# Bounding and masking the probabilities of the masked pairs in one VectorE instruction instead of two

## The reference

```python
scores = jnp.einsum('bhqd,bhkd->bhqk', q, k)          # q, k: 128 latent + 64 rotary
scores = jnp.clip(scores, -80.0, 80.0)
scores = jnp.where(causal[None, None], scores, -jnp.inf)
weights = jax.nn.softmax(scores / jnp.sqrt(jnp.float32(d_qk)), axis=-1)
attn = jnp.einsum('bhqk,bhkd->bhqd', weights, v)
out = attn.transpose(0, 2, 1, 3).reshape(B, S, H * D_H) @ W_O.T
```

## Time and profile before

| | |
|---|---|
| runs before, median of 3 | 1464.39 us (1462.96 to 1464.65) |
| the profiled execution's own time | 1462.57 us |
| its span | 1461.1 us |
| PE busy | 1387.2 us (95%), 9808 matmuls |
| DVE busy | 1173.1 us (80%), 1400 instructions |
| ACT busy | 769.9 us (53%) |
| POOL busy | 111.5 us (8%) |
| DVE, masked pairs: bounding L1177, mask L1181 | x64 each |

### The profile page before, as it was taken

The page is one execution under the profiler, slowest core; times in us unless marked ns, Lnnn a source line. Parts: engine busy times, 40 slices in busy tenths (PEclk is TensorE's granted clock), DMA queues, the critical chain, the costliest instruction groups (busy, mean ns, idle before and its releaser), DMA issues. The chain is left out here.

```text
span 1461.1 us, 27912 instructions
## 1 busy us (share of the span) xinstructions
PE 1387.2 (95%) x9808; PEld 1119.4 (77%) x9808; DVE 1173.1 (80%) x1400; ACT 769.9 (53%) x840; POOL 111.5 (8%) x150
## 2 busy tenths in 40 slices
PE   5999689999999999999999999999999999599998
PEld 4888567778777878787888878888788788378887
DVE  4666388898898898989889898898788798576764
ACT  3322356656666656565566655656655566432221
POOL 0000111101001000000010000000100000112211
PEclk9999899999999999999999999999999999899999
DMA  6423565544525333333242422422421611345652
GB/s 252 144 76 98 176 181 163 155 146 121 150 83 144 95 116 81 124 84 124 58 122 85 124 83 58 122 83 64 124 61 54 227 57 55 120 124 160 178 173 87
DMA packets 111949, 172.77 MB, mean 118 GB/s; under 512 B 9224, under 2 KB 68904, under 8 KB 109096
## 3 DMA queue, kind: packets, MB, share of 16 engines
q1 hardware_dynamic: 97528, 111.10, 24.6%
q0 software_dynamic: 13552, 59.60, 14.0%
q10 hardware_dynamic: 832, 1.57, 0.5%
HBM read 123.75 MB, written 48.50 MB: 118 GB/s over the span
## 5 line engine op out<-in xcount | busy, mean ns | idle before, releaser
L1094 ACT CAST prob_h<-prob 128x1024 fp32r<-128x1024 f32 (+1 forms) x288 | 289.6, 1005 | 271.8 <-DVE prob L1175 198.1
L1194 DVE TENSOR_TENSOR prob_l<-prob,prob_h 128x1024 fp32r<-128x1024 f32 (+1 forms) x288 | 335.9, 1166 | 39.6 <-ACT prob_h L1094 38.2
L1088 ACT ACTIVATE prob<-score_ps 128x1024 f32<-128x1024 f32 (+1 forms) x288 | 282.2, 980 | 149.1 <-PE score_ps L947 103.6
L947 PE MATMUL score_ps<-q_h,key_slot 64*128 64x512 f32 x1792 | 357.0, 392 | 3.7 <-DMA key_slot<-keys 3.5
L969 PE MATMUL out_ps<-prob_h,value_slot 64*128 64x512 f32 (+1 forms) x1792 | 341.7, 378 | 6.7 <-DVE prob_l L1194 5.1
L1189 DVE TENSOR_TENSOR total<-total,prob 128x1024 f32<-128x1024 f32 (+1 forms) x256 | 294.8, 1152 | 0.0
L969 PEld LDWEIGHTS out_ps<-prob_h,value_slot 64*128 64x128 f32 x1792 | 170.4, 184 | 54.9 <-DVE prob_l L1194 17.5
L1175 DVE TENSOR_SCALAR prob<-prob 128x1024 f32<-128x1024 f32 x224 | 155.1, 692 | 66.5 <-ACT prob L1088 66.5
L947 PEld LDWEIGHTS score_ps<-q_h,key_slot 64*128 64x128 f32 x1792 | 170.6, 184 | 43.6 <-issue 6.5
L947 PE MATMUL score_ps<-q_l,key_slot 64*128 64x512 f32 x896 | 177.3, 390 | 0.0
L947 PE MATMUL score_ps<-rot_hh,key_slot 64*128 64x512 f32 x896 | 177.2, 389 | 0.0
(11 more groups left out here) (193 smaller groups left out, 2022.7 us busy)
## 6 DMA issues: line engine op xcount, KB each, us to landing
key_slot<-keys SPq DMA_DIRECT2D x144, 256.0 KB, 2.7
value_slot<-values SPq DMA_DIRECT2D x144, 128.0 KB, 2.0
rows<-heads_rows SPq DMA_DIRECT2D x32, 512.0 KB, 5.9
rot_hh<-turned POOLq DMA_DIRECT2D x30, 512.0 KB, 6.1
heads_rows<-head_rows POOLq DMA_DIRECT2D x15, 1024.0 KB, 10.1
turned<-rot_hl POOLq DMA_DIRECT2D x14, 1024.0 KB, 5.1
rot_l<-turned POOLq DMA_DIRECT2D x30, 256.0 KB, 7.8
wo<-in_w_o POOLq DMA_DIRECT2D x1, 4096.0 KB, 13.0
```

What stands on the lines that cost most here:

```text
L947: mm = pe.matmul(score_ps[:, half, c * 512:(c + 1) * 512], keys_of[ROWS[r], :], moving[par][ROWS[r], half * HW + c * 512:half * HW + (c + ...
L1088: nc.scalar.activation(prob[half][:, 0:width], score_ps[:, half, 0:width], ACT.Exp, scale=QK_SCALE).then_inc(exp_done, 1)
L1094: nc.scalar.copy(prob_h[half][:, 0:width], prob[half][:, 0:width]).then_inc(high_done, 1)
L1194: nc.vector.tensor_tensor(p_l, p, p_h, ALU.subtract).then_inc(split, 1)
```

## The change

In CORNER and LATE pairs the bounding and the mask become one instruction: `scalar_tensor_tensor` computes min(max(p, P_MIN), limit), where `limit` is `keep.causal` broadcast over the four heads. For this `keep.causal` is filled with P_MAX instead of 1.0, so that it holds P_MAX where a key is seen and 0 where it is masked; min with it bounds from above and masks at once. In CORNER the instruction runs over all 256 tokens of each head (1024 columns), in LATE over the 128 tokens there are (512 columns). The semaphore `bounded` and the wait on it go. FULL pairs keep L1175.

```diff
-            nc.gpsimd.memset(keep.causal[:, :], 1.0).then_inc(cleared, 1)
+            nc.gpsimd.memset(keep.causal[:, :], P_MAX).then_inc(cleared, 1)
...
-        bounded = sem("bounded")
...
-                nc.vector.tensor_scalar(p, p, P_MIN, P_MAX, ALU.max, ALU.min).then_inc(bounded, 1)
-
-                dve.wait_ge(bounded, 4 * n + (2 if kind == LATE else 0) + half + 1)
-                masked = by_head(half, kind)[:, :, 0:P]
-                nc.vector.tensor_tensor(masked, masked, keep.causal[:, 0:P].unsqueeze(1).to_broadcast([P, HH, P]),
-                                        ALU.mult).then_inc(clipped, 1)
+                tokens = P if kind == LATE else CT
+                heads = by_head(half, kind)
+                limit = keep.causal[:, 0:tokens].unsqueeze(1).to_broadcast([P, HH, tokens])
+                nc.vector.scalar_tensor_tensor(out=heads, in0=heads, scalar=P_MIN, in1=limit,
+                                               op0=ALU.max, op1=ALU.min).then_inc(clipped, 1)
```

## The result

Ten runs of each kernel: median 1464.89 us before, 1459.11 us after. The ratio on record is 0.9955 (95% interval 0.9945 to 0.9965), 6.6 us less (5.1 to 8.1); the two medians are 5.8 us apart. Forecast were 7.4 us less and 1457.0 us.

What follows compares the result with a forecast made beforehand. PE was taken as the bound, with DVE's time counting only where PE stands still for it. The terms 3.4 + 3.6 + 0.4 = 7.4 us gave a median of 1457.0 us, range 1451.5 to 1461.5.

Steps and rivals of the forecast that it cites:

- Rivals B: The fused instruction runs at two columns a cycle, 692 ns in CORNER, giving 1453 us; chance 0.05.
- C: The fused instruction runs at half the rate, CORNER halves taking 2.29 us instead of 1.42, giving 1488 us; chance 0.03.
- Units 4 to 13: Ten units gain 0.36 us each, 3.6 us, through LATE's earlier halves and DVE's earlier row of work.
- the stop in LATE: PE's wait for `prob_l` in LATE's weighing, units 4 to 13, costing 0.34 us; it was to go.
- the large stop: PE's wait for `prob_l` at FULL k = 1 to 2, units 4 to 13; to end 0.35 us earlier, not much shorter.
- the CORNER saving is worth nothing by itself: In units 4 to 13 CORNER's 0.19 us a half brings nothing: PE is in the latent queries, DVE has pauses.
- Units 0 to 4: Few or no FULL pairs, at the pace of DVE and transfers: 3.4 us gained, bounds 1.3 and 5.5.
- The first term: Unit 0's CORNER and LATE halves, ahead of `split_turned`, become ready earlier, so unit 2 starts 1.27 us earlier.
- The smaller terms: CORNER in units 2 to 4 gives 1.1 us, DVE's lead in unit 2 0.4, LATE of units 2 and 3 0.34 and 0.2.
- Units 14 and 15: Latent queries behind CORNER come 0.38 us earlier in unit 14; unit 15's gain is lost at a key tile; 0.4 us.
- Rival A: Another wait hides the LATE gain in units 4 to 13: 4 us, 1460.4, or 2 us, 1462.4; chance 0.16.
- Rival D: Every 0.9 us that LATE saves in ten units moves the large stop: 12.8 us, 1451.6; chance 0.07.

Runs made afterwards that it cites:

- corner_split: The changed kernel, but CORNER uses two instructions on different columns, bounding the unmasked 512 and fused on the masked 512, with no wait; ratio 0.9964 against the kernel before.
- turn_on_act: The changed kernel with the rounding of the rotated queries moved from DVE to ACT in units 2 to 13; ratio 0.9906 against the kernel before.
- before_turn: The kernel before, without the fused instruction, with the rounding of the rotated queries moved from DVE to ACT in units 2 to 13; ratio 0.9948.
- after_weights: The changed kernel with the last phase's two weight loads issued later in unit 15, behind the store of unit 14's heads; ratio 0.9944 against the kernel before.
- before_again: The kernel before, unchanged, run once more for its profile alone; one run, 1467.17 us.
- before_weights: The kernel before with the last phase's two weight loads issued later in unit 15, behind the store of unit 14's heads; ratio 0.9998.
- corner_only: The kernel before with the fused instruction in CORNER pairs alone, LATE keeping two instructions with the wait; ratio 0.9992.

## Why the prediction was right, point by point

- **The instruction.** 1226 and 692 ns taken, 1224 and 684 measured. Rivals B (692 ns) and C (2290 ns) are out. The rows that decided between them were the two-input instructions and the small scalar_tensor_tensor of the earlier trace rows.
- **The wait between the two instructions.** The pair took 0.73 us from start to start in CORNER; two of that length without a wait between them are 0.61 apart. corner_split has the same at 512 columns: 0.34 us from start to start for a 0.42 us instruction, where before, with the wait, it was 0.45. So the trace disagrees once more with the rule of the Trainium skill (VectorE: DVE Perf Modes, "The DRAIN you can't avoid") that a semaphore costs nothing extra there. By that rule the sum was about 6 us. The interval of the measured time holds that too, so the rows decide it and not the whole time.
- **Units 4 to 13.** Forecast 3.6 us, measured 4.2 in the changed kernel, of which LATE alone is 3.7. The steps are shown: the stop in LATE goes, the large stop comes 0.33 us sooner and is no shorter, and it follows DVE's work (turn_on_act, before_turn). What I sized wrong is "the CORNER saving is worth nothing by itself": it is worth 1.5 us alone, in the odd units, and 0.5 beside the LATE saving.
- **Units 0 to 4.** Forecast 3.4 us. Between executions whose clock stayed up in unit 2, before took 116.35 us, after 112.97 and after_weights 112.31: 3.4 and 4.0 us less. The first term can be read by itself, as the end of `split_turned` of unit 0 after the first key tile. It was 25.88 us in before_again, before_weights and before_turn, 24.55 in after: 1.33 us, forecast 1.27. With LATE alone it was 24.95 (0.93 less). Before itself (25.20) and corner_only (24.80), both with less half clock at the start of unit 0 (3.0 us, 5.2 to 6.2 in the others), are 0.40 apart. These are the 2 x 0.45 and 2 x 0.19. Unit 2's first score matmul then came 40.29 us after the first key tile in after, 42.55 in before_again, 2.3 us sooner where 1.3 was forecast. What is more than 1.3 lies in the transfers (the store landed 5.1 us after its issue instead of 5.6), and they scatter: PE's wait for the queries was 1.8 to 3.0 us in the four profiles without the change and 1.7 to 3.2 in the seven with the whole change, so it can't be said to have fallen. The wait for `total` at the first sums did fall, from 1.7 to 3.0 us to 0 to 1.3; after, PE, as the earlier trace rows:
```profile
196.69 1.06 PE L901 MATMUL out_ps<-total,ones 128*32 128x512 f32 x8 [0.28 <-DVE total L1187]
```
  The smaller terms (1.1 for CORNER in units 2 to 4, 0.4, 0.34 and 0.2) are not confirmed one by one.
- **Units 14 and 15.** 0.4 us forecast for unit 14; the profiles with the change show 114.2 to 115.1 against 114.6 to 115.4, a scatter as large as the term. A gain within unit 15 is lost at the key tile: in its CORNER pair PE stood 1.63 us instead of 1.94, and then for the tile, whose load had been issued before that.
- **Rival A** took place in part: in even units PE now meets the key tile of k = 1 (the row at 512.50). It cost nothing, as argued, since DVE had begun its row of work. **Rival D** is out: the large stop gave back 0.33 us a unit, not 0.9.
- **The sum.** 7.4 us against 6.6 (5.1 to 8.1). Up to unit 15's sums the traces say more than that: 3.4 us (like clock with like), 4.2 and 0.4 (the means of the column 14-15, 115.1 and 114.7) are 8.0. Some 1.4 us seem to be given back behind them, or nothing, as the interval goes. Here the prediction put down nothing: "`combine` and the end are untouched". But "rest" is 209.94 us in after, and 209.5 in the mean of the seven profiles with the whole change (six of them 208.8 or more), against 208.0 to 208.5 in the four without it. So that the sum came within 1 us has some luck in it: units 4 to 13 were sized 0.6 too low, and what is lost behind was left out. The first waits of `combine` show it, after:
```profile
PEld merge_ps L1362 <- DVE merged_l L1462: 16.6, 5, 14.7
...
DVE rows L1420 <- POOL scale L1355: 30.7, 8, 12.3
```
The longest of them were 12.7 and 10.3 us before. They hang on the first transfers of `combine`, and over the seven profiles with the whole change they scatter (rest 208.1 to 211.6 us). Whether the change lengthens them, or the wait in unit 15, is open; no run was made for it.
- **The signs named in advance.** Counted from the first key tile, the sums of unit 5 came 3.9 us sooner in after than in before (3.7 forecast), those of unit 14 7.4 us (7 forecast).

## What to carry to other kernels

Two dependent instructions of an engine that is not the bound are worth fusing where a chain through that engine ends in a stop of the bound; count the stops, not the busy time. Of 18 us that DVE was relieved of, a third came through. Where the engine then works without a pause up to a later stop, that stop gives back what the start of its work gained (0.33 us here), and an instruction taken out between the two can count in full: one 0.69 us copy, moved to an engine with room, brought 7.3 us in the ten units in which the whole fusion brought 4.2. Before a difference between two profiles is put down to a change, take the unchanged one a second time, and compare stretch by stretch, each with its granted clock.

## What the runs showed of the hardware

- Here a burst delayed a small transfer that was issued after it. With the 4 MB load issued 5.1 us ahead, the 256 KB key tile of unit 15 landed 11.7 us after its issue in after (11.8 in before_again, 10.3 in before), where the median of all such tiles is 2.7 us. Pieces of 512 KB, one a pair, left no such wait.
- Such a wait can cost more than itself. In after PE stood 4.25 us; in the stretch with its end the granted clock was 0.62 of full speed, in the next 0.52, about the lower level of 1.2 GHz, and matmuls of 512 columns came every 0.43 us instead of 0.23 for some 4 us:
```profile
1144.00:1148.00 4.00, 1.44 (x6) 1.16 (x8) 0.48 (x1) 0.00 (x0) 0.00 (x0) 0.62 1.02 428
1148.00:1152.00 4.00, 4.00 (x28) 3.39 (x26) 0.00 (x0) 0.55 (x1) 0.00 (x0) 0.52 0.37 141
```
  (A stretch, its length, busy us and count of PE, PEld, DVE, ACT and POOL, the clock, the DMA share and GB/s.) It needn't happen: in after_weights PE stood 2.44 us and the clock stayed up, in before_weights it stood 2.54 us and 3.4 us at half followed. What decides it the runs don't show.
- The profiled stretches of steady work repeat within 0.3 us in 740 (once 0.8). The stretch with unit 2 scatters by up to 3.7 us in 115 for the same code, most of it because PE goes on at half clock after a stop in some executions and not in others. The stretch, not the whole time, is the place to measure an edit of a few tenths.
